# An attention and mixture-of-experts kernel: square roots on ScalarE, loads and routing moved, and the shared bank's products put between scores and values

## The reference, cut to what matters

```python
xn = (x - mean) / sqrt(var + 1e-5)              # first layer norm
p = xn @ Wv.T + bv                              # [4, 1024, 128], 16 heads of 8
scores = p_head @ p_head.T / sqrt(8)            # q = k = v = p
s = softmax(scores) @ p_head -> [4, 1024, 128] @ Wo.T + bo
z = layernorm(xn) * ln_g + ln_b                 # second layer norm, of xn
probs = softmax(z @ rW + rb); top 2 of 8, weights w = kept / sum
hid = gelu(z @ W1[e] + b1[e]);  mixed = sum_e w_e * (hid @ W2[e] + b2[e])
out = x + s * silu(xn + mixed)
```

## Time and profile before

| | |
|---|---|
| median of 3 runs | 629.43 us (628.19 to 631.27) |
| profiled execution | 632.46 us, span 630.7 us |
| TensorE busy | 571.2 us, 91% |
| ScalarE busy | 543.2 us, 86% |
| VectorE busy | 240.1 us, 38% |
| GpSimd busy | 230.1 us, 36% |
| mean granted TensorE clock | 0.936 of full |
| chain that ended last | TensorE 74%, ScalarE 9%, VectorE 7% of the span |

### The profile page before, as it was taken

One profiled execution on the slowest core, in us unless ns is written; L12 is line 12 of the kernel. 1 busy time (PEld: TensorE's weight loads), 2 busy tenths in 40 slices (PEclk: granted clock), 3 DMA queues, 4 the chain that ended last, 5 costly groups with the idle time before them and its releaser, 6 DMA issues.

```text
span 630.7 us, 11527 instructions
## 1 busy us (share of the span) xinstructions
PE 571.2 (91%) x3990; PEld 232.3 (37%) x3990; DVE 240.1 (38%) x695; ACT 543.2 (86%) x591; POOL 230.1 (36%) x252
## 2 busy tenths in 40 slices
PE   3778884799999999799999999999988999999996
PEld 2553320223344344333444344434334343433221
DVE  5553863573333333113222232223232852223381
ACT  4576663699999999979999999999999999999994
POOL 2364047827777774254211121112203334341000
PEclk9977776799999999869999999999995999999999
DMA  6137697746466655227363445453233654442220
GB/s 164 45 101 219 231 304 276 184 132 149 110 162 133 162 96 116 70 67 160 68 153 99 127 112 132 103 135 108 70 117 108 173 167 139 130 116 83 65 66 19
DMA packets 100989, 81.54 MB, mean 129 GB/s; under 512 B 54219, under 2 KB 92638, under 8 KB 100318
## 3 DMA queue, kind: packets, MB, share of 16 engines
q1 hardware_dynamic: 94270, 71.26, 43.2%
q0 software_dynamic: 6656, 9.48, 4.8%
HBM read 58.07 MB, written 28.39 MB: 137 GB/s over the span
## 4 chain that ended last, share of the span: by engine, by line
PE 74%; ACT 9%; DVE 7%; issue 5%; DMA 4%; SPq 1%; ACTq 0%; DVEq 0%
PE bank_v L1330 35%; PE pair L1276 16%; PE bank_f L1370 8%; PE bank_f L1379 8%; ACT exps L776 7%; DMA p_dram<-w_ring 3%; PE bank_f L1347 2%; PE pair L1236 1%; ACT pre L752 1%; PE bank_f L1343 1%; PE pair L1227 1%; DMA x_tok<-in_L_attn_x 1%; DVE o_turned L1082 1%; PE bank_f L1354 1%; DVE v_tok L863 1%
## 5 line engine op out<-in xcount | busy, mean ns | idle before, releaser
L776 ACT ACTIVATE exps<-pair 128x1024 f32<-128x1024 f32 x512 | 488.9, 1049 | 54.6 <-PE pair L1276 36.3
L1330 PE MATMUL bank_v<-exps,v_tok 128*32 128x512 f32 x2048 | 285.0, 630 | 3.1 <-ACT exps L776 1.6
L687 POOL DMA_INDIRECT o_dram<-o_ring,slot_place x80 | 77.4, 968 | 238.3 <-DVE o_ring L1133 238.0
L1276 PE MATMUL pair<-q_ring,k_ring 26*128 26x512 f32 x1024 | 152.9, 513 | 2.7 <-ACT exps L776 2.1
L1276 PEld LDWEIGHTS pair<-q_ring,k_ring 26*128 26x128 f32 x1024 | 60.7, 188 | 93.4 <-ACT exps L776 54.8
L672 POOL DMA_INDIRECT z_dram<-pre,dest_i x64 | 64.3, 1004 | 52.2 <-DVE place_i L1037 33.3
L1379 PEld LDWEIGHTS bank_f<-w_ring,pre 128*128 128x128 f32 x320 | 46.2, 208 | 72.2 <-issue 43.3
L1124 DVE TENSOR_TENSOR pre<-bank_f,w_ring 128x256 f32<-128x256 f32 x80 | 33.9, 423 | 102.1 <-PE bank_f L1370 102.1
L1379 PE MATMUL bank_f<-w_ring,pre 128*128 128x128 f32 x320 | 62.5, 322 | 9.7 <-ACT pre L752 5.3
L1133 DVE TENSOR_TENSOR o_ring<-bank_f,w_ring 128x128 f32<-128x128 f32 x80 | 23.2, 290 | 124.3 <-PE bank_f L1379 121.1
L679 POOL DMA_INDIRECT place_dram<-token_place,place_i x64 | 61.3, 958 | 19.5 <-issue 19.5
(11 more groups left out here) (154 smaller groups left out, 287.1 us busy)
## 6 DMA issues: line engine op xcount, KB each, us to landing
w_ring<-w_dram SPq DMA_DIRECT2D x80, 192.0 KB
w_ring<-w_dram SPq DMA_DIRECT2D x80, 129.0 KB
q_ring<-p_dram SPq DMA_DIRECT2D x56, 104.0 KB
k_ring<-p_dram SPq DMA_DIRECT2D x56, 96.0 KB
z_dram<-s_tok SPq DMA_DIRECT2D x4, 1280.0 KB, 13.1
z_ring<-z_dram SPq DMA_DIRECT2D x80, 64.0 KB
rows_in_sb<-o_dram SPq DMA_DIRECT2D x16, 256.0 KB, 2.9
p_dram<-z_ring SPq DMA_DIRECT2D x8, 256.0 KB, 2.9
```

What stands on the lines that cost most here:

```text
L687: pool.indirect_dma_start(o_dram[:, :], bass.IndirectOffsetOnAxis(slot_place[:, h, 4 * k + i:4 * k + i + 1].bitcast(U32), 0), o_ring[:, q ...
L776: nc.scalar.activation(exps[:, g % ES, 2 * half:2 * half + 2, :], pair[(2 * g + half) % 3][:, :, :], ACT.Exp, scale=SCALE).then_inc(exp_do ...
L1276: ins = nc.tensor.matmul(pair[h % 3][:, j % 2, :], k_ring[32 * j:32 * j + KROWS, n % 2, kt * P:(kt + 1) * P], q_ring[32 * j:32 * j + KROWS ...
L1330: ins = nc.tensor.matmul(bank_v[32 * j:32 * j + 32, :], v_tok[:, (n // HG) * KT + kt, first:first + 32], exps[:, g % ES, j, :], start=(kt ...
```

## The change

The diff, cut to its core, has these parts:

- **Roots.** ScalarE computes `Sqrt` of the variances (`root(c)`, four calls), VectorE makes the reciprocal and one Newton round (`invert`). The statistics are taken in whole groups (`take`), no longer between the steps of a root. `norm2` moves behind VectorE's branch, ahead of the main loop. ScalarE's first dummy activation is Sqrt, and an Exp one stands behind `project(7)`.
- **Early loads.** The third x chunk is loaded ahead of the small rows. Blocks 0 and 1 are stored to all four row groups (4 DMAs each), so that units 0 to 3 can be loaded by 8 DMAs each with no copy in DRAM; `load_unit(1)`, then `rb_bc`, `w1_stage` and `bo_bc` follow the last block's store. The copy in DRAM covers only blocks 2 to 7 and moves from step 2 to step 14.
- **Later routing.** Ranking, assignment and scatter of the first half move 4 steps back, `bias` (now 4 products of 4 columns) from step 4 to 22, `norm` from 12 to 27, the experts from 37 to 41. The second `scatter` moves from step 31 to 36, `zero_z(1)` from 12 to 8.
- **The order on TensorE** in a step: scores, bank products, values; before: scores, values, bank products.
- TensorE's second group of 4 warm-up products goes.

```diff
@@ constants
-RANK_AT = ((2, 3, 3, 4, 4, 5), (17, 18, 19, 20, 22, 23))
-COUNT_AT = (7, 24)
-ASSIGN_AT = ((7, 8, 8, 9, 10), (25, 26, 27, 28, 30))
...
-BIAS_AT = 4
-BIAS_COLS = 2
-NORM_AT = 12
-ZERO_AT = 12
...
-SCATTER_AT = (11, 31)
-MOE_AT = 37
+RANK_AT = ((6, 6, 7, 7, 8, 8), (17, 18, 19, 20, 22, 23))
+COUNT_AT = (11, 24)
+ASSIGN_AT = ((11, 12, 12, 13, 14), (25, 26, 27, 28, 30))
...
+BIAS_AT = 22
+COPY_HI_AT = 14
+BIAS_COLS = 4
+NORM_AT = 27
+ZERO_AT = 8
...
+SCATTER_AT = (15, 36)
+MOE_AT = 41
@@ timetable
-        place(("norm", g), NORM_AT + g - EARLY)
+        place(("norm", g), NORM_AT + (g - EARLY) * 3 // 2)
@@ sync, stores and first loads
             for g in range(NB):
                 tokens = slice(g * BLK, (g + 1) * BLK)
                 sp.wait_ge(parts_ready, g + 1)
-                for part in range(PARTS):
-                    row = (HI_ROW, LO_ROW)[part]
-                    sp.dma_start(p_dram[:, row:row + DK, tokens], (p_hi, p_lo)[part][:, g % 2, :]).then_inc(parts_stored[g % 2], 16)
+                hi_rows = (0, HI_ROW, LO_ROW + DK) if g < EARLY else (HI_ROW,)
+                for row in hi_rows:
+                    sp.dma_start(p_dram[:, row:row + DK, tokens], p_hi[:, g % 2, :]).then_inc(parts_stored[g % 2], 16)
+                sp.dma_start(p_dram[:, LO_ROW:LO_ROW + DK, tokens], p_lo[:, g % 2, :]).then_inc(parts_stored[g % 2], 16)
                 if g == EARLY:
                     for e in range(EARLY):
                         sp.wait_ge(n2_copied, e + 1)
                         sp.dma_start(p_dram[:, M_ROW, e * BLK:(e + 1) * BLK], m_blk[:, e, :]).then_inc(m_kept[0], 16)
-                    for i in range(2):
-                        sp.wait_ge(parts_stored[i], 16 * PARTS)
+                    for e in range(EARLY):
+                        sp.wait_ge(parts_stored[e], stored(e))
+                    sp.wait_ge(ring_cleared, 1)
+                    load_keys(0)
                     sp.wait_ge(m_kept[0], 16 * EARLY)
                     sp.wait_ge(m_zeroed, 32)
-                    sp.wait_ge(ring_cleared, 1)
-                    for j in range(4):
-                        load_head(0, 0, j, 0, kq_in[0])
-                        load_stabiliser(0, j, kq_in[0])
-                if g == 3:
...
+                    load_queries(0)
+            load_unit(1)
+            sp.dma_start(rb_bc[:, :], rb.rearrange("(a d) -> a d", a=1).broadcast_to([P, E])).then_inc(bias_in, 16)
+            sp.dma_start(w1_stage, W1.rearrange("e h f -> h e f")).then_inc(w1_staged, 16)
+            sp.dma_start(bo_bc[:, :], bo.rearrange("(a d) -> a d", a=1).broadcast_to([P, D])).then_inc(bias_in, 16)
+            zero_z(0)
@@ scalar
+            root(0)
             normalise(0)
             for s in range(NB + 1):
                 if s + 1 < NB:
                     normalise(s + 1)
+                if s == 0:
+                    root(1)
                 if s < NB:
                     copy_xT(s)
+                if 1 <= s < 3:
+                    root(s + 1)
                 if s >= 1:
                     project(s - 1)
+            act.wait_ge(act_dummy_ready, 1)
+            nc.scalar.activation(act_dummy[:, :], ident[0:1, 0:1], ACT.Exp).then_inc(act_dummy_ready, 1)
@@ vector
+            def invert(root, variance):
+                some = newton[:, 0:variance.shape[1]]
+                link(nc.vector.reciprocal(root, root))
+                link(nc.vector.scalar_tensor_tensor(out=some, in0=root, scalar=-0.5, in1=root, op0=ALU.mult, op1=ALU.mult))
+                link(nc.vector.tensor_tensor(some, some, variance, ALU.mult))
+                link(nc.vector.scalar_tensor_tensor(out=root, in0=some, scalar=1.5, in1=root, op0=ALU.add, op1=ALU.mult))
...
-            keep_p(0)
+            norm1(1, *NORMS[1])
+            take(16)
             norm1(2, *NORMS[2])
-            for g in range(1, NB):
+            variance2()
+            for g in range(NB):
                 keep_p(g)
...
-                elif g == 4:
-                    norm2()
...
+            norm2()
             keep_router_bias()
@@ tensor
-                keep_warm(WARM[1])
                 prologue()
-                first_scores(0)
                 rows_p(NB - 1)
-                first_scores(1)
-                first_scores(2)
+                for h in range(3):
+                    first_scores(h)
...
                     for half in range(2):
                         if 2 * g + half >= 3:
                             scores(g, half)
+                for use in USES.get(g, []):
+                    write_bank(*use)
                 if g >= VLAG:
                     values(g - VLAG)
-                for use in USES.get(g, []):
-                    write_bank(*use)
```

More of the change, by code:

```diff
@@ L41 @@
 PARTS = 2
+EARLY_PARTS = 4
 PROWS = 3 * DK
@@ L403, in _ @@
             load_x(1)
+            load_x(2)
             R = E * FC
@@ L410, in _ @@
             sp.dma_start(rw_sb[:, :], rW).then_inc(small_in, 16)
-            for c in range(2, len(X_CHUNKS)):
+            for c in range(3, len(X_CHUNKS)):
                 load_x(c)
@@ L479, in _ @@
             with sp.If(m2_bits > M2_LIMIT_BITS):
-                sp.wait_ge(kq_in[0], 16 * KQ_FIRST)
+                for i in range(2):
+                    sp.wait_ge(kq_in[i], 16 * KQ_LOADS)
                 with sp.Fori(0, NU // 2) as w:
@@ L705, in _ @@
             some = ident[:, 0:1]
-            nc.scalar.activation(act_dummy[:, :], ident[0:1, 0:1], ACT.Exp).then_inc(act_dummy_ready, 1)
+            nc.scalar.activation(act_dummy[:, :], ident[0:1, 0:1], ACT.Sqrt).then_inc(act_dummy_ready, 1)
             nc.scalar.activation(k_ring[:, :, :], some.unsqueeze(2).broadcast_to([P, 2, S]), ACT.Copy, bias=1.0, scale=0.0
@@ L717, in _, with root @@
             bv_col = cols[:, E * FC + 2:E * FC + 3]
+            def root(c):
+                act.wait_ge(variance_ready, c + 1)
+                if c < len(NORMS):
+                    some = slice(NORMS[c][0], NORMS[c][0] + NORMS[c][1])
+                    nc.scalar.activation(rstd[:, some], veps[:, some], ACT.Sqrt).then_inc(root_ready, 1)
+                else:
+                    nc.scalar.activation(rstd2[:, :], veps2, ACT.Sqrt).then_inc(root_ready, 1)
             def normalise(g):
@@ L824, in norm1 @@
                 link(ins)
-                link(nc.vector.tensor_scalar(veps[:, some], mv[:, some, 1], EPS, None, ALU.add), beside)
-                inverse_root(veps[:, some], rstd[:, some], beside)
+                nc.vector.tensor_scalar(veps[:, some], mv[:, some, 1], EPS, None, ALU.add).then_inc(variance_ready, 1)
+                if beside is not None:
+                    beside()
+                dve.wait_ge(root_ready, c + 1)
+                invert(rstd[:, some], veps[:, some])
                 nc.vector.scalar_tensor_tensor(out=shift[:, some], in0=mv[:, some, 0], scalar=-1.0, in1=rstd[:, some],
@@ L887, in keep_logits, with take @@
                 dve.wait_ge(logits_kept, h + 1)
-            def beside_norm(c):
-                if c == 0 and links[0] == 7:
-                    keep_m2()
-                else:
-                    statistics()
-            for t in range(7):
-                statistics()
-            link(statistics())
+            def take(count):
+                for _ in range(count):
+                    ins = statistics()
+                link(ins)
+            take(8)
             sum_gram()
-            norm1(0, *NORMS[0], lambda: beside_norm(0))
+            norm1(0, *NORMS[0], keep_m2)
             router_weights()
-            norm1(1, *NORMS[1], statistics)
-            assert statistics() is None
-            keep_p(0)
+            take(8)
+            norm1(1, *NORMS[1])
+            take(16)
             norm1(2, *NORMS[2])
-            for g in range(1, NB):
+            variance2()
+            for g in range(NB):
                 keep_p(g)
```

103 lines of the change are left out of this document (46 added, 57 removed).

## The result

The changed kernel takes 673.99 us (median; 673.61 to 680.28), the one before 630.12 beside it (628.19 to 631.27): a ratio of 1.072, with 95% interval 1.065 to 1.079. The forecast was 642 with a range of 608 to 660: slower, as forecast, but by 44 us and not by 13. The profiled execution's span is 672.0 us against 630.7.

What follows compares the result with a forecast made beforehand. TensorE was taken to bound the main stage. Span: 133.7 (step 38) + (630.7 - 152.85) + 30.6 + 1.4 = 643.5, so +12.8; added to the median 629.43 this gives 642 us, range 608 to 660.

Steps and rivals of the forecast that it cites:

- Part 1: Roots and prologue: earlier roots and loads bring the first exponential at about 42 us, against 52.73.
- Part 2: VectorE late for the loop: new stall of about 13 us; step 22's scores still at 98.3, 25 us gained.
- rows 6: Profile rows before the change, 60 to 124 us: waits for the norm rows' stores, 12.8 us, forecast as gone.
- Part 3: Steps 22 to 38: 35.4 us against 29.3 before, 6.1 lost, with two collisions adding 2.6.
- The collisions: At turns of `bank_v`, VectorE reads the product behind the turn, so the next product stalls 1.45 or 1.32 us.
- Part 4: Order scores, product, values: TensorE's own time unchanged, but stalls at 22 steps from 41 to 225 cost 30.6 us.
- two turns of z: At steps 49 and 121 a `turn_z` follows the late read: 2 x 0.7 us.
- B: Rival, faster: the bank collision costs nothing, 608 us; chance 0.16.
- C: Rival, no change: VectorE on time, the 13 us stall doesn't come, the collision does, 629 us; chance 0.12.
- D: Rival, slower still: granted clock falls to about half for a step after each stall, up to 688 us; chance 0.06.

Runs made afterwards that it cites:

- x6: Changed kernel with the two bias rows' loads at the start, right behind the router weights: 661.52 us, ratio 1.046.
- x2: Changed kernel with the old order on TensorE (scores, values, products): 641.88 us, ratio 1.018.
- x8: Changed kernel with old order and three moves (W2's copies at step 19, bias loads at the start, W1's store two steps later): 613.47 us, ratio 0.970.
- x7: Changed kernel with the 1 MB store of W1's scaled copy two steps later: 672.10 us, ratio 1.065.
- x4: Changed kernel with W2's copies and the places' clearing at step 19 instead of 38: 663.58 us, ratio 1.055.
- x11: x8 with the first z load issued three steps earlier and the first half's row additions one step later: 606.00 us, ratio 0.960.
- x3: Changed kernel, new order kept, but VectorE reads the product before it turns `bank_v`: 648.54 us, ratio 1.027.
- x10: Changed kernel, new order kept, with VectorE's read ahead of the turn and the same three moves as x8: 619.60 us, ratio 0.982.
- x1: Kernel before with the new order in all steps but 89 and 186: 663.61 us, ratio 1.055.

## Why the prediction was right in kind and wrong in size

The forecast span was 643.5 us, the measured one 672.0: 28.5 us are missing. By its own steps:

- **Part 1 (roots and prologue): the sum right, with luck in it.** First exponential 41.59 against 42, and ScalarE normalised from 11.79 (said: 11.8). But TensorE began its blocks at 16.25, not at 14.5 (15.99 before), though `m2` was done 1.2 us sooner (10.59), and unit 0's last load was issued by 38.45, not 37.6; its scores started 2.6 us behind that, where I had counted on 3.4. The table load of 1.28 us stood ahead of the exponential. The Trainium skill's 1.38 us of drain per change of set (ScalarE: Activation LUTs, "What ACT_TABLE_LOAD costs") does not show: the load starts at 39.20 and the next activation at 40.50.
- **Part 2 (VectorE late): right in mechanism, its size partly by luck.** `rconst` at 64.18 (said: about 62), `o_turned` begun at 72.13 and done at 72.84 (73.2), step 22's scores at 96.59 (98.3). x6 shows the cause. But two errors cancel: the bias row landed 7.6 us behind its issue where 5.6 was priced, and from `rconst` to the end of `chosen` it took 8.0 us (to 72.21) where 10.3 was priced. The part gained 1.7 us more than said. **Wrong in it:** "the 12.8 us of rows 6 are gone". The wait of a norm's read for its stores was not gone but at another place: 4.76 us on VectorE, 7.20 on ScalarE.
- **Part 3 (steps 22 to 38): the step that failed first.** From 96.59 to 140.51 it took 43.9 us in place of 35.4: 8.5 missing. I priced TensorE's slots at the full clock, and not the queue: I did not place the norms' stores behind W1's, nor allow for a lower clock (0.88 in the stretch). The collisions are not it: x2, which has none, takes 47.1 at a clock of 0.75. The three moves take 11.3 us off the stretch between x2 and x8, whose 35.8 is still 3.0 above what the forecast has without its two collisions. Alone, W1's store gives 2.3 (x7), the biases 2.1 (x6: 41.7) and W2's copies 0.4 (x4: 43.4); how the rest divides between the clock (0.75 in x2, 0.90 in x8) and the moves together is open.
- **Steps 38 to 44, the largest miss.** They took 31.4 us against 13.4, of which I had priced one collision (1.45): 16.6 missing. The sum took everything between step 38 and the end as in the kernel before, plus collisions. But `keep_w2` and `clear_places` hang on `SCATTER_AT[1] + 2`, which the diff moves from step 33 to 38, and `load_z(0)` comes at `MOE_AT - 3`, also step 38, with these ahead of it in SyncE's program. Twelve issues of about 1 us each stood there to be read in the diff's constants. x4 gave 10.4 us of it back. The eight weight loads ahead of them had moved too: `MOE_AT - 8 + 2 * q` became `MOE_AT - 6 + 2 * q`, steps 29 and 31 became 35 and 37. x4 leaves them there and still waits 5.27; x11, which puts z's load ahead of them and makes the other moves, waits 1.51.
- **Part 4 (the order): right.** Said: 22 stalls of 1.4, 30.6 us and 1.4 for two turns of z, and 147 exponentials in the window. The first stall lies in step 42; measured between steps 44 and 232, the other 21 turns take 75.1 us in place of x2's 44.7, so 30.4, with z's turns in it. (The timetable before has a product in 174 of the 193 steps from 38 to 230, not in 178; the sum doesn't use it.) The stretch is 35.4 longer than before, 4.9 more than forecast, and step 198 alone is 4.3 of that (6.4 us in place of 2.1). This again is a queue: the rows' loads came behind the unit's, `LOAD_AT` having moved with `MOE_AT` but the unit's load not. x11, which adds the rows one step later, has 1.8 there.
- **That the order as such costs nothing** held for a plain step: 2.07 against 2.07. Over the whole kernel it did not: with the stalls taken away x3 and x10 are still 6.7 and 6.1 us behind x2 and x8, for which the forecast had no term. By the Trainium skill a change of tiling mode drains TensorE (TensorEngine Tiling (Array Packing), "Key Properties"); both orders change it three times a step, and the trace shows no difference between them.
- **Rivals:** B is out (145 in the window, x1), C is out (step 11's wait, x6), D is out (clock 1.00 in the window).

The misses add up: -1.7 + 8.5 + 16.6 + 4.9 + 0.2 (tail) = 28.5. The largest by far, the one at step 198 and part of the 8.5 are waits for transfers that the new timetable put behind others in SyncE's queue. So the step of the prediction that failed is its sum's assumption that, behind step 22, the change costs TensorE's slots and collisions alone: the norm waits "gone", the rest as before. Waits for transfers that the new timetable makes late stood in it at nothing. The range failed with it: its upper end was built from the stalls that were priced, and a further wait in a queue was nowhere in it.

## What to carry to other kernels

When a timetable is shifted, list for each queue the transfers in their new order and what stands directly ahead of the first one that somebody waits for: here moving three of them turned the 642 us of the changed kernel with the old order into 613, and two more moves made it 606. When two engines share a bank, follow the order of reads on the reader too: a reader that first waits for something else hands that wait to the writer. It is paid at every turn once the next write is due soon behind what the reader waits for: here 0.44 us behind the end of the values, where it had been 2.08. A change that bundles a gain and a loss is worth taking apart before it is judged: all of it but the order, with the three moves, is worth 17 us (x8 against the kernel before), and the order costs 32. What makes up the 17 us was not taken apart. By the table x8 leads by 10.4 us at step 0, by 35.4 at step 22 and by 17.5 at step 232, so more was gained between steps 0 and 22, from where bias and norm products were moved away, than by the earlier start; no run separates the roots, the loads and the later routing.

## What was not expected of the hardware

A small transfer issued right behind a large one landed late, by an amount that varied. The norms' stores of 123.00, behind the 1 MB store of 121.78, let VectorE go only at 130.80. VectorE's wait for them was 4.8 us here, and 4.1, 5.2, 2.3 and 2.1 in x2, x3, x4 and x6, which have the same order of stores; in x7, with nothing large ahead, there was none. The bias row shows less of this: issued at 56.4, half a microsecond behind W1's 1 MB load, it landed 7.6 us later (by the trace's row of that tile); 1.4 us behind the same load, in the kernel before, it took 5.6, and at the start of the kernel, in x6, 5.4. So about 2 of the 12 us that x6 gained are a slow landing, and the rest is the row's place in SyncE's queue.

An issue in SyncE's queue took about 1 us for the expert weights, whose address the code first loads (8.29 us for 8), and for the broadcast rows of W2's bias (7.72 for 8), against 0.4 for the units' loads (1.62 for 4): so it was 8.29 + 3.19 + 7.72 + 1.06 us of issuing that stood ahead of z.
